# Two-step top-p graph kernel on one core: query projections set apart from the key projections, the last normalisation rounds spread over the last body, and step two's kept sums taken from a column of ones

## The chip, the core and the metric

One core of a Trainium2 chip runs the kernel. TensorE (PE), VectorE (DVE), ScalarE (ACT), GpSimd (POOL) and SyncE (SP, which issues the DMAs) each work through a stream of their own in program order and meet through semaphores. The metric is device time in microseconds (us), as a median of several runs. Lower is better.

## What is computed

The input x has 3327 rows of 128 features, adj is 3327 by 3327. Cut to what matters:

```python
def _top_p_attention(X, W1, W2, W3):
    q = X @ W1.T @ W2.T
    k = X @ W3.T
    probs = softmax(q @ k.T)                 # one row for each node
    # sort, keep the largest until their sum before them reaches 0.9
    A = probs * mask
    return A / jnp.maximum(A.sum(-1, keepdims=True), 1e-12)

R = S + eye(N); R = R / R.sum(-1, keepdims=True)
Xf = Xa = X
for n in range(2):
    A = _top_p_attention(Xa, W1, W2, W3)
    Xf = R @ Xf
    Xa = A @ Xa
    Z = Z + Xf @ U1[n].T + Xa @ U2[n].T
h = X + Z
y = (h - mean(h)) / sqrt(var(h) + 1e-5) * ln_g + ln_b
out = layernorm(x + y)
```

## The kernel before

The 3327 rows are 26 tiles of 128 and 13 pairs of tiles. A row of attention or of adj is 3328 columns wide, in 7 chunks of 512 (the last is 256). All is fp32.

**The preamble** (L549 to L565 on TensorE, L660 to L671 on ScalarE, L1155 to L1165 on VectorE) takes the features chunk by chunk. TensorE turns a chunk (L532), ScalarE copies it into `xT`, which is the tile `blkT` under another name with room for two chunks (L665). TensorE multiplies it by the key weights (L558) and by the query weights (L559). VectorE copies the keys into `kT` (L1159) and the queries into `Q`, in two halves (L1162). TensorE then makes the logits of pair 0 for the chunk before (L546, in banks 6 and 7 every time) and ScalarE stores them (L657). VectorE reads runs of them with MAX8 (L821); when all are read it takes the negated row maximum (L844, L846), and with that ScalarE starts on the exponentials (L678 for the candidates, L683 for the rows). Ahead of them in ScalarE's stream lies the copy of the turned U weights (L671), which TensorE turns at L569. Only the queries of the first chunk are read by pair 0.

**The bodies.** A unit is one tile of 128 rows of A or R times the features: 7 chunks, each turned by TensorE (L585), copied to `blkT` by ScalarE (`empty_block`, L708) and multiplied (L606), two chunks behind in step two. A body holds the two A units of a pair and some R units. TensorE's and ScalarE's streams walk through the bodies in the same order (`for b in bodies`), and the logits and exponentials of a later pair lie between the chunks of a body. Pair p's body can start when VectorE has masked its first tile.

**VectorE, pair by pair:** it waits for the exponentials, searches the threshold (`search`, L917 first), finds the ties, masks each of the two tiles (`settle`: four L1212 and one L1214, which also gives the kept sum), then takes the maximum of the kept sums with a least value (L1262) and the reciprocal (L1263). ScalarE scales with that when it empties the sums of an A unit (`store_sums`, L729), and GpSimd adds the result to `H` (`add_part`, L479). GpSimd also adds the diagonal to each loaded adj tile (L443), and finishes the R units of step one (`save`, with an inverse at L454 to L457 and a scaling at L467).

**The end.** The two layer norms of a pair are six rounds that alternate between ScalarE and GpSimd (`norm_round`; L756, L758, L760 on ScalarE, L487 to L501 on GpSimd). ScalarE does rounds at chunk 2 of a unit. The rounds that are left when the last body starts are four, all of pair 11: rounds 2 to 5. Before, ScalarE does all four ahead of the first copy of the last body, and then loads the table of the square root (L772). Rounds 2 and 5 are L760; after round 2 GpSimd runs L499, L500 and L501. The last pair's tiles are finished by VectorE (L1291 to L1301) with a square root on ScalarE for each norm (L795).

## Time and profile before

| | before |
|---|---|
| median of 3 runs | 1452.03 us (1451.74 to 1453.0) |
| the profiled execution | 1454.91 us |
| its span, first to last instruction | 1452.9 us |
| mean granted TensorE clock | 0.93 |
| PE busy | 1232.3 us, 85% |
| DVE busy | 1290.2 us, 89% |
| ACT busy | 921.8 us, 63% |
| POOL busy | 354.6 us, 24% |

A busy share is an average over stages that have different limits. The step-one bodies run from about 43 to 414 us, step two's bodies from about 531 us to the end. In the timeline a row gives the start, the duration, the engine, the line, the operation and how many instructions are merged; in brackets stands how long the engine had idled, and what it waited for. In the chain of work that ended last only the part of an instruction that nothing later covers is counted.

### The profile page before, as it was taken

The page shows a single profiled execution, that of the slowest core. Times are in us where ns is not written, and L with a number is a line of the kernel's source. Part 1 is how long each engine was busy: PE and PEld are TensorE (multiplying, and loading weights), DVE is VectorE, ACT ScalarE, POOL GpSimd, SP SyncE. Part 2 cuts the span into 40 slices and gives each one's busy share as a digit, 9 for nine tenths or more (in the row PEclk, how much of TensorE's full clock was granted, in tenths as well). Part 3 has the DMA queues.
Part 4 walks back from the last instruction along what each step waited for, and adds up shares of the span by engine and source line. Part 5 has one row for each costly group of instructions (what it writes and reads, how often), then busy time and mean ns, then how long its engine had stood idle before and what let it go on. Part 6 is the DMA issues. An engine that isn't in the chain of part 4 may idle for free.

```text
span 1452.9 us, 29724 instructions
## 1 busy us (share of the span) xinstructions
PE 1232.3 (85%) x9162; PEld 1039.4 (72%) x9162; DVE 1290.2 (89%) x7002; ACT 921.8 (63%) x1974; POOL 354.6 (24%) x584
## 2 busy tenths in 40 slices
PE   8799999999997979997999888839894938749875
PEld 3577777777785978887887777637874837647875
DVE  5789898989985899999989999999999989999992
ACT  3787888788757565655566646546765627556743
POOL 0221132123201331412132121102331314202340
PEclk9899999999998989998999898959997979969997
DMA  5000000000021541412223131402221121302230
GB/s 201 1 2 2 2 2 2 2 2 2 2 96 48 186 146 48 142 49 95 96 96 119 25 143 49 142 1 83 108 95 50 48 95 49 142 2 95 96 88 8
DMA packets 16599, 96.49 MB, mean 66 GB/s; under 512 B 1251, under 2 KB 8930, under 8 KB 9730
## 3 DMA queue, kind: packets, MB, share of 16 engines
q1 hardware_dynamic: 16384, 94.14, 18.5%
q8 instruction: 72, 1.18, 0.3%
q14 instruction: 143, 1.17, 0.3%
HBM read 92.43 MB, written 1.70 MB: 65 GB/s over the span
## 4 chain that ended last, share of the span: by engine, by line
PE 43%; DVE 37%; ACT 12%; issue 5%; POOL 2%; DVEq 1%; DMA 0%; SPq 0%; ACTq 0%; POOLq 0%
PE bank L606 24%; DVE cand L821 14%; PE bank L585 11%; DVE junkC L878 8%; PE bank L546 5%; ACT E L683 5%; ACT blkT L708 2%; DVE E L1212 2%; ACT cand L678 2%; DVE sub L1042 2%; DVE E L1214 1%; PE bank L621 1%; DVE junkS L878 1%; DVE slots L941 1%; ACT S L683 1%
## 5 line engine op out<-in xcount | busy, mean ns | idle before, releaser
L708 ACT ACTIVATE blkT<-bank 128x512 f32<-128x512 f32 (+1 forms) x728 | 406.8, 565 | 291.2 <-PE bank L585 287.3
L821 DVE MAX8 cand<-E 128x8 f32<-128x32 f32 (+1 forms) x2992 | 405.0, 192 | 36.6 <-ACT E L657 21.5
L606 PEld LDWEIGHTS bank<-X,blkT 128*128 128x128 f32 x2704 | 330.6, 192 | 112.0 <-ACT blkT L708 78.3
L606 PE MATMUL bank<-X,blkT 128*128 128x129 f32 (+1 forms) x2704 | 377.7, 282 | 17.4 <-ACT blkT L708 16.3
L585 PE MATMUL bank<-ident,S 128*128 128x128 f32 x1560 | 242.5, 275 | 16.3 <-POOL S L443 16.3
L585 PE MATMUL bank<-ident,E 128*128 128x128 f32 x1144 | 182.0, 283 | 84.2 <-DVE E L1214 84.2
L878 DVE SCALAR_TENSOR_TENSOR junkC<-cand,st 128x128 f32<-128x128 f32 (+2 forms) x390 | 243.3, 632 | 2.4
L606 PE MATMUL bank<-YF,blkT 128*128 128x128 f32 x1352 | 192.8, 287 | 40.6 <-ACT blkT L708 40.5
L606 PEld LDWEIGHTS bank<-YF,blkT 128*128 128x128 f32 x1352 | 172.3, 199 | 72.3 <-ACT blkT L708 61.2
L546 PE MATMUL bank<-kT,Q 64*128 64x512 f32 (+1 forms) x728 | 198.8, 616 | 8.2 <-ACT E L657 7.6
L585 PEld LDWEIGHTS bank<-ident,E 128*128 128x128 f32 x1144 | 142.7, 147 | 86.5 <-DVE E L1214 85.4
L585 PEld LDWEIGHTS bank<-ident,S 128*128 128x128 f32 x1560 | 186.7, 142 | 21.2 <-POOL S L443 18.4
L606 PE MATMUL bank<-YA,blkT 128*128 128x128 f32 x1352 | 187.4, 282 | 13.9 <-ACT blkT L708 13.9
L657 ACT ACTIVATE E<-bank 128x512 f32<-128x512 f32 (+1 forms) x308 | 158.2, 567 | 62.4 <-PE bank L546 61.9
L606 PEld LDWEIGHTS bank<-YA,blkT 128*128 128x128 f32 x1352 | 172.3, 199 | 14.8 <-issue 13.2
L1214 DVE SCALAR_TENSOR_TENSOR E<-E,st 128x3328 f32<-128x3328 f32 x44 | 163.6, 3733 | 8.8 <-DVE flag_i L1019 6.8
L683 ACT ACTIVATE E<-E,negm 128x1664 f32<-128x1664 f32 x88 | 147.5, 1677 | 0.0
L472 POOL TENSOR_TENSOR H<-hy,H 128x128 f32<-128x128 f32 x26 | 38.8, 1492 | 281.3 <-ACT hy L744 281.3
L1212 DVE MATCH_REPLACE8 E<-gone,E 128x832 f32<-128x832 f32 x104 | 103.8, 1009 | 0.0
L678 ACT ACTIVATE cand<-cand,negm 128x520 f32<-128x520 f32 (+1 forms) x78 | 45.0, 592 | 90.8 <-DVE negm L846 90.8
L546 PEld LDWEIGHTS bank<-kT,Q 64*128 64x128 f32 x728 | 57.2, 186 | 43.3 <-issue 27.6
L479 POOL TENSOR_TENSOR H<-part_h,H 128x128 f32<-128x128 f32 x50 | 33.8, 677 | 192.4 <-ACT part_h L729 192.4
(220 smaller groups left out, 1338.2 us busy)
## 6 DMA issues: line engine op xcount, KB each, us to landing
S<-in_adj_dram SPq DMA_DIRECT2D x50, 1663.5 KB, 7.0
S<-in_adj_dram SPq DMA_DIRECT2D x2, 1455.6 KB, 8.8
X<-in_x_dram SPq DMA_DIRECT2D x6, 256.0 KB, 4.8
out_dram<-H SPq DMA_DIRECT2D x1, 1408.0 KB
S<-in_adj_dram SPq DMA_DIRECT2D x2, 194.9 KB, 10.1
u_in<-in_L_gnn_U_dram SPq DMA_DIRECT2D x4, 64.0 KB, 9.6
out_dram<-H SPq DMA_DIRECT2D x1, 128.0 KB
w_in<-in_L_gnn_W_dram SPq DMA_DIRECT2D x2, 32.0 KB, 2.1
```

Of the source, the lines that this page charges most:

```text
L472: pool.tensor_tensor(H[:, u.t, :], hy[:, z, 0:D], H[:, u.t, :], ALU.add)
L546: pe.matmul(lg_banks(q)[xx][:, 0:LW[c]], Q[h0:h1, p, :], kT[h0:h1, s, c * BANK:c * BANK + LW[c]], start=True, stop=True).then_inc(logits_r ...
L585: m = pe.transpose(BLK[early][slot][:, b * P:(b + 1) * P], src[:, j * P:(j + 1) * P], ident[:, :])
L606: m = pe.matmul(bank[int(u.acc)][:, 0:width], blkT[:, slot, b * P:(b + 1) * P], rhs[:, j, 0:width], start=(j == 0), stop=(j == NT - 1))
L657: act.activation(E[where_e[s, p]][:, xx, c * BANK:c * BANK + LW[c]], lg_banks(q)[xx][:, 0:LW[c]], ACT.Copy).then_inc(logits_done, 1)
L678: act.activation(c, c, ACT.Exp, bias=negm[:, par, xx:xx + 1], scale=1.0, accum_out=total[:, par, xx:xx + 1])
L683: return act.activation(e[:, xx, lo:hi], e[:, xx, lo:hi], ACT.Exp, bias=negm[:, par, xx:xx + 1], scale=1.0, accum_out=Zh[:, par, xx, half: ...
L708: act.activation(blkT[:, slot, 0:w], BLK[early][slot][:, 0:w], ACT.Copy).then_inc(blk_done, 1)
L821: v.max(cand[:, par, xx, 8 * r:8 * r + 8], E[where_e[self.s, self.p]][:, xx, r * w:min((r + 1) * w, N)]).then_inc(s_max, 1)
L878: return v.scalar_tensor_tensor(out=out, in0=a, scalar=limit, in1=a, op0=ALU.is_lt, op1=ALU.mult, accum_out=total)
L1212: link.post(v.match_replace(back, gone[:, xx, k, :], back, 0.0))
L1214: v.scalar_tensor_tensor(out=e[:, xx, :], in0=e[:, xx, :], scalar=one(TSTAR, xx), in1=e[:, xx, :], op0=ALU.is_ge, op1=ALU.mult, accum_out= ...
```

## The change

Three things change.

1. In the preamble `xT` becomes a tile for all chunks (it takes the room of `YF`, not used before step one's bodies). Only chunk 0 is multiplied by the query weights at once; the other six are multiplied after the last logits of pair 0, into banks 0 to 5, and VectorE copies them after it has read the last run of pair 0. Pair 0's logits alternate between two pairs of banks. TensorE starts the bodies after the copies.
2. The four rounds of the last body are done by ScalarE behind the copies and sums of steps 0, 3, 6 and 9 of the last body's 14 chunks, and the square root's table is loaded at step 12.
3. `YA` gets a column of ones, and A units of step two (but for the last pair) multiply 129 columns. ScalarE copies sum and kept sum unscaled; GpSimd takes the maximum, the inverse (four instructions), scales the 128 columns and adds. VectorE no longer reads out the kept sum in step two and drops L1262 and L1263 there, but for the last pair. The least value goes into a tile of its own, `least`, before whose rewriting VectorE waits for `h_taken`.

```diff
-        YA = sb("YA", [P, NT, D])
+        YA = sb("YA", [P, NT, D + 1])
...
-        xT = blkT
+        xT = YF[:, :, :].rearrange("p t d -> p (t d)")
...
-        FIRST_LG = [bank[6], bank[7]]
+        FIRST_LG = [[bank[6], bank[7]], [bank[1], bank[3]]]
...
+            pool.memset(YA[:, :, D:D + 1], 1.0).then_inc(setup_done, 1)
...
             def add_part(u):
                 pool.wait_ge(sums_ready, u.k + 1)
                 if u.m:
                     pool.wait_ge(h_taken, u.m)
-                pool.tensor_tensor(H[:, u.t, :], part_h[:, u.m % 2, :], H[:, u.t, :], ALU.add).then_inc(h_taken, 1)
+                ps = part_h[:, u.m % 2, 0:D]
+                if u.kind == "A":
+                    total, d = part_h[:, u.m % 2, D:D + 1], sum_inv[:, u.x:u.x + 1]
+                    then(pool.tensor_scalar(total, total, least[:, (NPAIR + u.pair) % 2, u.x:u.x + 1], None, ALU.max))
+                    inverse(d, total)
+                    then(pool.tensor_scalar(ps, ps, d, None, ALU.mult))
+                pool.tensor_tensor(H[:, u.t, :], ps, H[:, u.t, :], ALU.add).then_inc(h_taken, 1)
...
-                pe.matmul(bank[2 * (c % 2)][:, 0:w], W3T2[:, :, :], xT[:, c % 2, 0:w], start=True, stop=True)
-                pe.matmul(bank[2 * (c % 2) + 1][:, 0:w], WqT2[:, :, :], xT[:, c % 2, 0:w],
-                          start=True, stop=True).then_inc(kq_ready, 1)
-                if c:
-                    pe.wait_ge(kq_done, 3 * c)
+                k = pe.matmul(bank[2 * (c % 2)][:, 0:w], W3T2[:, :, :], xT[:, c * BANK:c * BANK + w], start=True, stop=True)
+                if c == 0:
+                    pe.matmul(bank[1][:, 0:w], WqT2[:, :, :], xT[:, 0:w], start=True, stop=True).then_inc(kq_ready, 1)
+                else:
+                    k.then_inc(kq_ready, 1)
+                    pe.wait_ge(kq_done, c + 2)
                     logits(0, 0, c - 1)
...
+            pe.wait_ge(logits_done, 2 * NCH)
+            for c in range(1, NCH):
+                pe.matmul(bank[c - 1][:, 0:CW[c]], WqT2[:, :, :], xT[:, c * BANK:c * BANK + CW[c]],
+                          start=True, stop=True).then_inc(q_ready, 1)
             pe.wait_ge(u_loaded, 64)
-            pe.wait_ge(logits_done, 2 * NCH)
             for n in range(2 * STEPS):
                 last = pe.transpose(bank[7][:, n * P:(n + 1) * P], u_in[:, n, :], ident[:, :])
             last.then_inc(u_turned, 1)
-            pe.wait_ge(setup_done, 14)
+            pe.wait_ge(setup_done, 15)
+            pe.wait_ge(q_done, 2 * (NCH - 1))
...
             def multiply(g):
-                width = D + 1 if u.s == 0 and u.kind == "R" else D
+                width = D + 1 if (u.s == 0) == (u.kind == "R") and u.k <= last_part.k else D
...
             def store_sums(u):
-                if u.kind == "A":
-                    gp = u.s * NPAIR + u.pair
-                    act.wait_ge(inv_ready, gp + 1)
-                    scale = a_inv[:, gp % 2, u.x:u.x + 1]
+                if u.kind == "A" and u.s == 0:
+                    act.wait_ge(inv_ready, u.pair + 1)
+                    scale = a_inv[:, u.pair % 2, u.x:u.x + 1]
...
+                elif u.kind == "A":
+                    ins = act.activation(part_h[:, u.m % 2, :], ps[:, 0:D + 1], ACT.Copy)
...
             for b in bodies:
                 if b.p == NPAIR - 1 and b.s:
-                    for job in norm_rounds.get(last_part.k + 1, ()):
-                        norm_round(*job)
-                    act.wait_ge(act_round, 2 * len(norm_at))
-                    act.activation(junkA[:, 0, 0:1], ones[:, 0:1], ACT.Sqrt)
+                    for n, job in enumerate(norm_rounds.get(last_part.k + 1, ())):
+                        b.late.setdefault(len(b.seqs) - 2 - LATE_EVERY * (len(norm_rounds[last_part.k + 1]) - n), []).append(job)
...
+                    for job in b.late.get(m, ()):
+                        norm_round(*job)
+                    if b.late and m == len(b.seqs) - 2:
+                        act.wait_ge(act_round, 2 * len(norm_at))
+                        act.activation(junkA[:, 0, 0:1], ones[:, 0:1], ACT.Sqrt)
...
             def search(link, s, p, par):
+                if s and p >= 2:
+                    dve.wait_ge(h_taken, a_unit[s, 2 * (p - 2) + 1].m + 1)
+                link.post(v.tensor_scalar(least[:, par, :], z, 1e-12, None, ALU.mult))
...
+            runs.finish()
+            for c in range(1, NCH):
+                dve.wait_ge(q_ready, c)
+                queries(c, bank[c - 1], q_done)
...
+                            if s and p < NPAIR - 1:
+                                v.scalar_tensor_tensor(out=e[:, xx, :], in0=e[:, xx, :], scalar=one(TSTAR, xx), in1=e[:, xx, :],
+                                                       op0=ALU.is_ge, op1=ALU.mult).then_inc(a_ready, 1)
...
+                    if s == 0 or p == NPAIR - 1:
                         link = Chain(s_tie)
...
                         link(v.tensor_tensor(two(SUM), two(SUM), least[:, par, :], ALU.max))
                         v.reciprocal(a_inv[:, par, :], two(SUM)).then_inc(inv_ready, 1)
```

`queries` is the pair of query copies that stood in the preamble's loop.

## Rows read from the trace of the kernel before

**Rows 1.** The page's chain that ended last, shares of the span by engine.
```profile
PE 43%; DVE 37%; ACT 12%; issue 5%; POOL 2%; DVEq 1%; DMA 0%; SPq 0%; ACTq 0%; POOLq 0%
```
**Rows 2.** Busy by stretch: from:to length, then busy us and instructions by engine, PEclk, DMA.
```profile
74.00:102.00 28.00, 27.68 (x196) 20.89 (x195) 26.25 (x122) 22.59 (x46) 8.64 (x8) 1.00 0.01 2
...
676.00:744.00 68.00, 65.01 (x504) 57.64 (x502) 62.68 (x375) 42.12 (x84) 17.93 (x30) 0.96 0.28 99
...
1214.00:1300.00 86.00, 57.13 (x447) 50.47 (x446) 82.02 (x456) 46.36 (x111) 21.12 (x40) 0.84 0.17 61
```
**Rows 3.** The chain in order of time, 845 to 1300 us: start, us, what.
```profile
968.50 2.82 PE bank L585 x12
...
1291.89 2.82 PE bank L585 x12
```
**Rows 4.** Timeline of PE in the preamble: start, us, instruction, and idle before.
```profile
17.18 1.13 PE L546 MATMUL bank<-kT,Q 64*128 64x512 f32 x4
...
19.60 1.02 PE L559 MATMUL bank<-blkT,WqT 128*128 128x512 f32 x2
20.55 1.13 PE L546 MATMUL bank<-kT,Q 64*128 64x512 f32 x4
...
31.09 1.09 PE L546 MATMUL bank<-kT,Q 64*128 64x255 f32 x4 [0.60 <-DVE Q L1162]
32.74 0.63 PE L569 MATMUL bank<-ident,u_in 128*128 128x128 f32 x4 [0.56 <-ACT E L657]
```
**Rows 5.** Timeline of ACT around the first exponentials.
```profile
33.40 0.60 ACT L671 ACTIVATE UT<-bank 128x512 f32<-128x512 f32 x1 [0.81 <-PE bank L569]
35.48 0.40 ACT L678 ACTIVATE cand<-cand,negm 128x128 f32<-128x128 f32 x1 [1.48 <-DVE negm L846]
...
42.92 0.57 ACT L708 ACTIVATE blkT<-bank 128x512 f32<-128x512 f32 x1
```
**Rows 6.** Timeline of DVE at the end of the preamble.
```profile
31.03 3.96 DVE L821 MAX8 cand<-E 128x8 f32<-128x208 f32 x14
```
**Rows 7.** Busy by stretch as in rows 2, after the first exponentials' idle time.
```profile
38.50:49.00 10.50, 5.46 (x18) 3.62 (x19) 4.94 (x33) 8.48 (x14) 0.00 (x0) 0.53 0.00 1
```
**Rows 8.** Timeline of DVE where pair 9 ends and pair 10 begins.
```profile
1210.49 3.69 DVE L1214 SCALAR_TENSOR_TENSOR E<-E,st 128x3328 f32<-128x3328 f32 x1
...
1214.76 0.16 DVE L917 TENSOR_TENSOR st<-Zh 128x2 f32<-128x2 f32 x1
```
**Rows 9.** Timeline of DVE where pair 8 ends and pair 9 begins.
```profile
1125.46 0.50 DVE L1262 TENSOR_TENSOR st<-st 128x2 f32<-128x2 f32 x1
```
**Rows 10.** GpSimd lines: count, then duration in ns as min/median/max.
```profile
L454 POOL TENSOR_TENSOR row_inv<-new_x,minus_one x26: 562/569/2478, 61.1 to 853.7; 128x1 f32<-128x1 f32 x26
...
L467 POOL TENSOR_SCALAR scaled<-hy,row_inv x26: 612/612/3295, 64.7 to 857.0; 128x128 f32<-128x128 f32 x26
```
**Rows 11.** Timeline of ACT from the last part's sums to the end.
```profile
1408.99 0.37 ACT L729 ACTIVATE part_h<-bank,row_inv 128x128 f32<-128x128 f32 x1 [1.65 <-PE bank L606]
...
1421.07 1.28 ACT L772 ACT_TABLE_LOAD   x1
...
1422.47 1.55 ACT L708 ACTIVATE blkT<-bank 128x512 f32<-128x512 f32 x3
...
1440.02 0.19 ACT L795 ACTIVATE sd<-sd 128x1 f32<-128x1 f32 x1
```
**Rows 12.** Timeline of PE in the last body.
```profile
1423.19 2.04 PE L606 MATMUL bank<-YA,blkT 128*128 128x128 f32 x8 [12.99 <-ACT blkT L708]
...
1432.22 1.06 PE L606 MATMUL bank<-YA,blkT 128*128 128x128 f32 x8
...
1433.55 0.61 PE L606 MATMUL bank<-YA,blkT 128*128 128x128 f32 x4
...
1439.54 2.40 PE L606 MATMUL bank<-YA,blkT 128*128 128x128 f32 x20
```
**Rows 13.** Timeline of POOL between the parts of the last norm rounds.
```profile
1411.00 3.98 POOL L500 TENSOR_TENSOR H<-H,gb 128x256 f32<-128x256 f32 x1
```

More of the change, by code:

```diff
@@ L113, in new_body @@
         b.early, b.s, b.p, b.off = early, s, p, off
-        b.units, b.seqs, b.emit, b.exps, b.turn, b.mul, b.first_exps = [], [], {}, {}, {}, {}, []
+        b.units, b.seqs, b.emit, b.exps, b.turn, b.mul, b.first_exps, b.late = [], [], {}, {}, {}, {}, [], {}
         b.look = 1 if early else 2
@@ L181, in gnn_top_p_kernel @@
     ROUNDS = 6
+    LATE_EVERY = 3
     norm_rounds = {}
@@ L234, in gnn_top_p_kernel @@
         blkT = sb("blkT", [P, 3, BANK])
-        xT = blkT
+        xT = YF[:, :, :].rearrange("p t d -> p (t d)")
         new_x = sb("new_x", [P, 2, D + 1])
-        part_h = sb("part_h", [P, 2, D])
+        part_h = sb("part_h", [P, 2, D + 1])
+        least = sb("least", [P, 2, 2])
+        sum_inv = sb("sum_inv", [P, 2])
         scaled = sb("scaled", [P, D])
@@ L316, in gnn_top_p_kernel @@
         kq_done = sem("kq_done")
+        q_ready = sem("q_ready")
+        q_done = sem("q_done")
         kq_next = sem("kq_next")
@@ L357, in lg_banks @@
             if q < NCH:
-                return FIRST_LG
+                return FIRST_LG[q % 2]
             ring = LG[0] if q < late_logits else LG[1]
@@ L536, in logits @@
                 q = lg_seq(s, p, c)
-                before = q - (1 if q < NCH or q >= late_logits else 2)
+                before = q - (1 if q >= late_logits else 2)
                 if q in (NCH, NCH + 1):
@@ L899, in smallest_kept, with search @@
                 return w, d
-            def search(link, s, par):
+            def search(link, s, p, par):
                 n = NC[s]
@@ L1149, in drop_ties, with queries @@
                 link(v.memset(excess[:, xx, :], 0.0))
-            dve.wait_ge(setup_done, 14)
+            def queries(c, q_ps, done):
+                m = CW[c] // (2 * P)
+                for xx in range(2):
+                    h0, h1 = xx * DA, (xx + 1) * DA
+                    v.tensor_copy(Q[h0:h1, 2 * c:2 * c + m, :],
+                                  q_ps[h0:h1, 0:CW[c]].rearrange("p (m x d) -> p m x d", x=2, d=P)[:, :, xx, :]).then_inc(done, 1)
+            dve.wait_ge(setup_done, 15)
             dve.sem_clear(s_max)
@@ L1179, in _ @@
                     link = Chain(s_search, runs, fill, 8 if s else 0)
-                    search(link, s, par)
+                    search(link, s, p, par)
                     if p + 1 < NPAIR:
@@ L1213, in settle @@
                                 dve.wait_ge(s_tie, link.n)
-                            v.scalar_tensor_tensor(out=e[:, xx, :], in0=e[:, xx, :], scalar=one(TSTAR, xx), in1=e[:, xx, :],
-                                                   op0=ALU.is_ge, op1=ALU.mult, accum_out=one(SUM, xx)).then_inc(a_ready, 1)
+                            if s and p < NPAIR - 1:
+                                v.scalar_tensor_tensor(out=e[:, xx, :], in0=e[:, xx, :], scalar=one(TSTAR, xx), in1=e[:, xx, :],
+                                                       op0=ALU.is_ge, op1=ALU.mult).then_inc(a_ready, 1)
+                            else:
+                                v.scalar_tensor_tensor(out=e[:, xx, :], in0=e[:, xx, :], scalar=one(TSTAR, xx), in1=e[:, xx, :],
+                                                       op0=ALU.is_ge, op1=ALU.mult, accum_out=one(SUM, xx)).then_inc(a_ready, 1)
                     with dve.If(code < 1):
@@ L1256, in _ @@
                             settle()
-                    link = Chain(s_tie)
-                    if gp >= 2:
-                        q = gp - 2
-                        dve.wait_ge(sums_ready, a_unit[q // NPAIR, 2 * (q % NPAIR) + 1].k + 1)
-                    dve.wait_ge(a_ready, 2 * gp + 2)
-                    link(v.tensor_tensor(two(SUM), two(SUM), two(LEAST), ALU.max))
-                    v.reciprocal(a_inv[:, par, :], two(SUM)).then_inc(inv_ready, 1)
+                    if s == 0 or p == NPAIR - 1:
+                        link = Chain(s_tie)
+                        if gp >= 2:
+                            dve.wait_ge(sums_ready, a_unit[0, 2 * min(gp - 2, NPAIR - 2) + 1].k + 1)
+                        dve.wait_ge(a_ready, 2 * gp + 2)
+                        link(v.tensor_tensor(two(SUM), two(SUM), least[:, par, :], ALU.max))
+                        v.reciprocal(a_inv[:, par, :], two(SUM)).then_inc(inv_ready, 1)
             link = Chain(s_fin)
```

28 lines of the change are left out of this document (11 added, 17 removed).

## The prediction

> **What bounds the kernel now.** I read the chain of work that ended last first, then busy time by stretch, then the chain in order of time, and then the two ends instruction by instruction. The page's chain is shared between PE (43%), DVE (37%) and ACT (12%) [rows 1]: no engine bounds the kernel alone, so each part of the change is worth what the stage around it lets through. Busy time by stretch tells the stages apart [rows 2]. In a step-one body (74 to 102 us) PE is busy 27.68 of 28 us; these bodies repeat and nothing of them is changed. In the early bodies of step two (676 to 744) PE and DVE are both near 95%, and the chain there runs through TensorE and the exponentials that its order puts ahead of block copies. In a late body (1214 to 1300) DVE is busy 82 of 86 us and PE only 57. The chain in order of time [rows 3] gives the joints of that late stretch: VectorE up to 968.5, where TensorE at last gets pair 6's first masked tile; then a body of TensorE and the exponentials it leads to; VectorE again from the next search until 1291.9, where TensorE gets pair 10's first tile; and from there TensorE without a longer wait, until the last body, where it stands still for 12.99 us [rows 12].
>
> **The preamble.** A chunk now takes 3.37 us of TensorE, from one logits start to the next (17.18 to 20.55) [rows 4], and the query product with its gap is 0.95 of it (19.60 to 20.55). Without it I take 0.9 less. The first removed product lies ahead of 13.8 us, five more full ones and a half one ahead of the last logits: about 0.8 + 4 x 0.9 + 0.7 for the chunk edges = 5.1, plus the 0.60 us that the last logits waited for VectorE's query copy [rows 4]. So the last logits start near 25.5 instead of 31.09, the reading of the last runs (14 MAX8, 3.96 us [rows 6]) ends near 29.5, and the maximum is there 5 to 6 us sooner. Does ScalarE start the exponentials then? Not yet, because the copy of the U weights stands ahead of them in its stream, and TensorE makes that only behind the moved products. Before: last logits 31.09, U turned from 32.74, copied from 33.40 to 34.0, then 1.48 us of waiting for the maximum, first exponential at 35.48 [rows 4, 5]. After: last logits 25.5, stored by 26.7 to 26.8 (the same 1.6 us later), six products of 0.86, the last one half: 4.7 us, to 31.5; U turned and copied 1.3 us later, to 32.8. The exponentials start at about 32.8 and not at 35.48: **2.7 us**, rounded down to 2.6. What was removed is thus half given back; the wait that ends last is the U copy. The six pairs of query copies (5 x 0.87 + 0.6 = 4.9 us, of the kind now beside the key copies) run on VectorE from about 29.6 to 34.6 while ScalarE takes 7.44 us for the exponentials (35.48 to 42.92 [rows 5]); VectorE would idle there. TensorE's four filling jobs, which end before the exponentials with room now, start at 34.6 and end near 38.5, and the first block copy is due at 40.2. Bounds: 1.0 (the loop is held by ScalarE or VectorE at some chunk, whose copies and MAX8 add up to an estimated 1.7 and 1.9 to 2.4 us a chunk against 2.5 for TensorE) and 5.0 (if the U copy were no obstacle).
>
> **The clock behind it.** Between 38.5 and 49 us the granted clock is 0.53, that is 1.2 GHz, after TensorE idled for the exponentials, and its 5.46 us of work there are on the chain [rows 7]; at 2.4 GHz they would be 2.7. In the new order it idles in two shorter pieces, 32.0 to 34.6 for the query copies and about 1.7 us before the first block copy. Whether the clock stays up over such pieces this trace doesn't settle, so I take under half, **1.2 us**, with bounds of -1 (low clock during the filling jobs, which then end after the exponentials) and 2.7.
>
> **Step one and the early bodies of step two.** They move earlier as they are: 0. The memset of 26 ones is one more in a row of small ones before the features arrive. The 129th column is in step one's R units now; I cost it at nothing, since a tile's product there and in A units takes the same 0.22 us, with 0.4 us (24 units x 26 tiles x 4 passes of one column at 2.4 GHz is 1.0 us, less than half of it on the chain) as upper bound.
>
> **VectorE in step two.** From the end of a pair's second masking (1210.49 + 3.69 = 1214.18) to the first instruction of the next search (1214.76) are 0.58 us with L1262 and L1263 in them [rows 8]; I leave 0.13 for the semaphores, so 0.45 a pair. It counts only where VectorE carries the chain: by rows 3 that is the end of pair 5, and of pairs 8 and 9; the other ends have their slack in front of a wait on TensorE or ScalarE. 3 x 0.45 = 1.35, and 0.3 more where GpSimd had stretched L1262 to 0.50 us [rows 9]. The masking itself stays at 3.69 us for 3328 elements, 1.1 ns each; dropping its accumulator is at most the read-out, which another instruction covers. On GpSimd each of 24 A units gets a maximum, four instructions of inverse and a scaling: in its usual durations 0.2 + 0.57 + 3 x 0.19 + 0.61 + 6 gaps of 0.08 = 2.4 us [rows 10], beside 8.7 us per unit. They take something back on VectorE, about what is seen where both run: -0.35 over the 8 or so A units within VectorE's part of the chain. Sum: **1.3 us**, bounds -1 and 3.5. The wait for `h_taken` before `least` is rewritten has search's later instructions queued behind it, but it asks for the sums of two pairs ago: 0. `store_sums` loses its wait for the inverse, which came long before: 0.
>
> On that contention the Trainium skill ("GPSIMD Engine Reference", the table at its head) says that GpSimd shares its SBUF interfaces with VectorE and contends with VectorE instructions that have two SBUF inputs. The trace agrees: L1262 has two such inputs and took 0.50 us beside GpSimd's L499 [rows 9], and GpSimd's L500 took 3.98 us beside the last masking [rows 13]. It is the rule that speaks against this part of the change.
>
> **The end.** Now ScalarE empties the last part at 1408.99, does four rounds in turn with GpSimd, and loads the table (1421.07); the first block copies come at 1422.47 [rows 11], and TensorE, which had turned three chunks, multiplies from 1423.19 [rows 12]. Put aside, the copies start at 1409.3 and TensorE multiplies from 1409.9. At the high clock a chunk costs 1.33 us (1432.22 to 1433.55 [rows 12]): 0.89 of products and 0.44 of turning. What is left is 12 x 0.89 + 2 x 0.45 of products and 9 x 0.44 + 2 x 0.22 of turning = 16.0, so TensorE ends at 1425.9 instead of 1439.54 + 2.40 = 1441.94: 16.0 us sooner. (Before, the restart at low clock cost 2.9 of it.) Two things come off. The square root's table (1421.07 to 1422.47, 1.40 us) now lies between the last block copy and the first square root, which today follows the last copy at once (1440.02) and starts VectorE's serial end: -1.4. And the rounds sit among the copies. Round 2 goes behind copy 2, near 1411; GpSimd's three instructions after it end between 1414.3 and 1415.7, as the last masking may hold L500 [rows 13]; round 3 stands behind copy 5, near 1414.5, so ScalarE waits up to a microsecond and does 0.8 us of work, and copy 6, needed at 1417.7, still comes in time. Round 5 meets the same at copy 11 and delays copies 12 and 13 by 0 to 0.9. I take -0.6. The second A tile is masked at 1414.4 and asked for at 1416. The output DMA of the pairs up to 11 leaves near 1423, against an end near 1438. So **14.0 us**, bounds 9 (each round's wait comes through to TensorE, 2 us at two places, and the last copies late) and 15.5.
>
> The Trainium skill ("ScalarE: Activation LUTs", What ACT_TABLE_LOAD costs) gives some 2.66 us for a switch of tables with what follows it; by that the end would be worth 12.7. The trace shows 1.28 for the load and the next copy 1.40 us after its start [rows 11], which I use.
>
> **Sum.** 2.6 + 1.2 + 1.3 + 14.0 = 19.1 us. The profiled execution took 1454.91 us, so it would be 1435.8. The median of the runs shown is 2.9 us lower, and on it the forecast is 1452.03 - 19.1 = **1432.9 us**.
>
> **Rivals.**
> - The end gives less: ScalarE, in order, waits for GpSimd at rounds 3 and 5, TensorE and the last copies come late. For it: L500 at 3.98 us against a usual 0.73, and a masking that lies just there; against it: the ring of three blocks, two chunks of slack. 4 to 5 us less: 1437.4.
> - The start gives nothing: the U copy and a low clock during the filling jobs eat the 3.8 us. For it: U's copy behind 4.7 us of products; against it: the 7.4 us of exponentials hide the copies. 1436.7.
> - VectorE gains more than the small instructions. The Trainium skill ("Vector Engine (DVE) Microarchitecture Reference", Points that are easy to get wrong) says that this form of instruction with two fp32 inputs runs at half throughput, none of the ports being left for the accumulator's read-out. If the accumulator halved the masking's rate, a masking without it would be 1.8 us shorter, and 8 of them lie on VectorE's part of the chain: 14.4 more, 1418.5. Against it: 3.69 us for 3328 elements is 1.1 ns each, and MAX8 with one input takes 3.96 / (14 x 208) = 1.4 ns [rows 6, 8]; so the masking doesn't run at half a rate.
> - Slower: GpSimd becomes the bound. If its seven instructions per A unit are each held by VectorE's long ones, as L454, L467 and L500 are at worst (2.48, 3.30, 3.98 us), a unit's part takes over the 8.7 us that TensorE needs for a unit, and the next adj tile's diagonal and the norm rounds, queued behind, stop TensorE and ScalarE. It decides from 8.7 us per unit; at 1 us lost on each of 24 units it eats the gain, at 1.8 the time is 1452 - 19 + 43 = 1476. Against it: medians of 0.57 and 0.61 [rows 10] and POOL idle for most of the time [rows 2].
> - The change does nothing that counts: 1452.
>
> **How the numbers follow.** Forecast as summed, within 3 us: 0.56. End gives less 0.16, start gives nothing 0.12, more gain by clock or VectorE 0.10, GpSimd as bound 0.03, no effect 0.03. The range runs from 1428.5 (clock at its bound, VectorE and the end near theirs) to 1438.5 (one of the first two rivals). What a measurement of this kernel can tell from no change is about 0.2%, 2.9 us. Faster 0.95, same 0.02, slower 0.03.
>
> **What would show it.** In the profile after: logits 2.5 us apart, first exponential at 32.8 with ScalarE's U copy just before it; no or a shorter stretch of low clock at 40 to 49; L917 0.15 us after the last masking; the last body's copies 1.33 us apart directly behind the last part's sums, the table load right behind the last of them, and no clock drop. The prediction is wrong if TensorE waits for a block copy in the last body, if VectorE's maskings get shorter, or if TensorE's waits for GpSimd's diagonal grow.

## The result and the profile after

| | before | after |
|---|---|---|
| median of 4 runs, taken side by side | 1452.51 us (1451.74 to 1455.0) | 1439.34 us (1438.29 to 1440.45) |
| ratio, 95% interval | | 0.9906 [0.9889, 0.9924] |
| span of the profiled execution | 1452.9 us | 1438.7 us |
| PE / DVE / ACT / POOL busy, us | 1232.3 / 1290.2 / 921.8 / 354.6 | 1232.8 / 1289.1 / 919.2 / 445.5 |

The kernel became faster by 13.2 us; 19.1 were forecast, and 1439.3 lies above the range. The page of after, its chain by engine and two of its groups:

```profile
PE 43%; DVE 37%; ACT 12%; issue 5%; POOL 2%; DVEq 1%; DMA 0%; SPq 0%; ACTq 0%; POOLq 0%
...
L1248 DVE SCALAR_TENSOR_TENSOR E<-E,st 128x3328 f32<-128x3328 f32 x24 | 88.9, 3703 | 0.9
...
L1251 DVE SCALAR_TENSOR_TENSOR E<-E,st 128x3328 f32<-128x3328 f32 x20 | 74.5, 3760 | 7.9 <-DVE flag_i L1044 6.8
```

The chain has the same shares as before [rows 1]. L1248 is the masking without the accumulator, L1251 the one with it: mean 3703 and 3760 ns, so the rate did not change.

**The start.** Timelines of after, PE then ACT (start, us, instruction, idle before):

```profile
17.61 1.13 PE L560 MATMUL bank<-kT,Q 64*128 64x512 f32 x4
...
20.12 1.13 PE L560 MATMUL bank<-kT,Q 64*128 64x512 f32 x4
...
26.95 4.99 PE L584 MATMUL bank<-YF,WqT 128*128 128x512 f32 x12 [1.29 <-ACT E L677]
31.77 0.60 PE L588 MATMUL bank<-ident,u_in 128*128 128x128 f32 x4
```
```profile
25.26 1.64 ACT L677 ACTIVATE E<-bank 128x512 f32<-128x512 f32 x4 [0.60 <-PE bank L560]
32.41 0.60 ACT L689 ACTIVATE UT<-bank 128x512 f32<-128x512 f32 x1 [5.52 <-PE bank L588]
32.91 0.39 ACT L696 ACTIVATE cand<-cand,negm 128x128 f32<-128x128 f32 x1
...
40.33 0.58 ACT L726 ACTIVATE blkT<-bank 128x512 f32<-128x512 f32 x1
```

A chunk takes 2.51 us instead of 3.37, the exponentials start at 32.91 instead of 35.48, and the first block copy comes at 40.33 instead of 42.92 [rows 4, 5].

Not all of that is the change. Up to the second chunk's key product both kernels have the same TensorE stream, and yet it starts at 12.01 us in before and at 11.30 in after. Timelines of PE, before and then after:

```profile
9.52 1.91 PE L559 MATMUL bank<-blkT,WqT 128*128 128x512 f32 x2
...
12.01 1.02 PE L558 MATMUL bank<-blkT,W3T 128*128 128x512 f32 x2
```
```profile
9.57 1.46 PE L574 MATMUL bank<-YF,WqT 128*128 128x512 f32 x2
...
11.30 1.02 PE L572 MATMUL bank<-YF,W3T 128*128 128x512 f32 x2
```

The first pairs of products take up to 2.08 us where later ones take 1.02, and how many do so differs from execution to execution. From that key product the first exponential comes 23.47 or 23.48 us later in all four traces with the old preamble (before and the experiments e3, e4 and e9 below) and 21.41 to 21.61 us later in the nine others with the new one (e5, whose preamble differs, aside). So the change makes the start 1.9 us shorter, and 0.7 us of the difference between these two traces is luck.

**The last body.** Timeline of ACT in after, from the last part's sums:

```profile
1408.83 0.37 ACT L748 ACTIVATE part_h<-bank,row_inv 128x128 f32<-128x128 f32 x1 [1.65 <-PE bank L626]
1409.21 1.57 ACT L726 ACTIVATE blkT<-bank 128x512 f32<-128x512 f32 x3
1412.24 0.88 ACT L779 ACTIVATE H<-H,shift,rs 128x128 f32<-128x128 f32 x2 [1.46 <-POOL shift L509]
...
1423.97 0.38 ACT L726 ACTIVATE blkT<-bank 128x256 f32<-128x256 f32 x1 [0.51 <-PE bank L605]
1424.37 1.28 ACT L812 ACT_TABLE_LOAD   x1
1425.66 0.20 ACT L812 ACTIVATE u_in<-ones 128x1 f32<-128x1 f32 x1
1425.78 0.19 ACT L818 ACTIVATE sd<-sd 128x1 f32<-128x1 f32 x1
```

The first square root comes 16.95 us behind the last part's sums (1425.78 - 1408.83). Before it came 31.03 behind (1440.02 - 1408.99 [rows 11]). From it to the end are 12.9 us in both. So the end gave 14.08 us, which is 31.03 less 16.95. But the last part's sums themselves come only 0.16 us sooner: all that the start and the kept sums brought is gone by then.

There is room left in the end. Timeline of DVE in after:

```profile
1420.03 0.15 DVE L1320 TENSOR_SCALAR sd<-sd 128x1 f32<-128x1 f32 x1
1425.99 0.17 DVE L1332 RECIPROCAL rs<-sd 128x1 f32<-128x1 f32 x1 [5.81 <-ACT sd L818]
```

VectorE has the first tile's variance at 1420.18 and idles 5.81 us for its square root, which stands behind all block copies and the table in ScalarE's stream.

**Where it went.** I set the unit sums of the two traces side by side (the lead is the time in before less that in after, for the same instruction). At the second search the lead is 3.75 us (73.19 to 69.44). It then falls in three steps of 1.6 to 1.7 us. Besides these, 0.7 us go between 457 and 543 us, and the lead swings between 1080 and 1220 us and comes out of that 1.0 us larger. Two of the steps are falls of the granted clock at places where the trace of before has none. Busy by stretch of after (columns as in [rows 2]); before shows 1.00 in the last column but two of all four:

```profile
386.00:390.00 4.00, 2.29 (x15) 1.99 (x16) 3.16 (x18) 2.99 (x6) 1.13 (x1) 0.92 0.00 0
390.00:394.00 4.00, 4.00 (x18) 2.80 (x17) 3.68 (x26) 1.73 (x5) 0.73 (x2) 0.66 0.01 4
1342.00:1346.00 4.00, 1.97 (x14) 1.78 (x13) 3.86 (x31) 0.69 (x2) 2.30 (x8) 0.88 0.78 253
1346.00:1350.00 4.00, 4.00 (x27) 4.00 (x27) 3.96 (x8) 2.00 (x4) 0.43 (x1) 0.69 0.43 179
```

The lead goes from 3.8 to 2.2 over the first and from 2.5 to 0.8 over the second. The third step, from 1.1 to -0.6, is a wait at 1388 us. Timelines of after, POOL then PE:

```profile
1383.85 0.70 POOL L515 TENSOR_TENSOR H<-H,X 128x256 f32<-128x256 f32 x1
1384.54 0.30 POOL L490 TENSOR_SCALAR part_h<-part_h,least 128x1 f32<-128x1 f32 x1
1384.92 0.68 POOL L461 TENSOR_TENSOR sum_inv<-part_h,minus_one 128x1 f32<-128x1 f32 x1
...
1386.59 0.69 POOL L492 TENSOR_SCALAR part_h<-part_h,sum_inv 128x128 f32<-128x128 f32 x1
1387.37 0.45 POOL L493 TENSOR_TENSOR H<-part_h,H 128x128 f32<-128x128 f32 x1
1387.79 0.22 POOL L501 TENSOR_SCALAR mv<-mv 128x2 f32<-128x2 f32 x1
1387.97 0.46 POOL L450 TENSOR_TENSOR S<-S,ident 128x128 f32<-128x128 f32 x1
```
```profile
1388.48 0.66 PE L605 MATMUL bank<-ident,S 128*128 128x128 f32 x4 [1.51 <-POOL S L450]
```

GpSimd's new work for an A unit (2.8 us, from 1384.54 to 1387.37), itself queued behind a norm round (up to L515), stands ahead of the next adj tile's diagonal (L450), and TensorE waits for that. TensorE's next wait of this kind, for the last adj tile, gives 0.8 us back (1.18 us in after, 1.95 in before). It does so with no loss ahead of it too: e1, e2 and e3 gain 0.7 to 0.8 us on before there, so it is before's trace that has the long wait.

### The profile page after: what moved, and what is told of

It is laid out like the page before. It is cut to its first block, busy times and chain, and to the rows that moved or that the text cites. A ratio compares the mean times of both kernels' runs of the same rounds, so it can differ in the third digit from the quotient of the medians.

```text
span 1438.7 us, 29788 instructions
## 1 busy us (share of the span) xinstructions
PE 1232.8 (86%) x9162; PEld 1040.7 (72%) x9162; DVE 1289.1 (90%) x6954; ACT 919.2 (64%) x1974; POOL 445.5 (31%) x729
## 3 DMA queue, kind: packets, MB, share of 16 engines
q8 instruction: 72, 1.18, 0.3%
## 4 chain that ended last, share of the span: by engine, by line
PE 43%; DVE 37%; ACT 12%; issue 5%; POOL 2%; DVEq 1%; DMA 0%; SPq 0%; ACTq 0%; POOLq 0%
PE bank L626 24%; DVE cand L844 13%; PE bank L605 11%; DVE junkC L901 8%; PE bank L560 5%; ACT E L701 5%; ACT blkT L726 2%; DVE E L1245 2%; ACT cand L696 2%; DVE sub L1067 2%; DVE E L1248 1%; PE bank L641 1%; DVE junkS L901 1%; DVE slots L966 1%; DVE st L909 1%
## 5 line engine op out<-in xcount | busy, mean ns | idle before, releaser
L626 PE MATMUL bank<-YA,blkT 128*128 128x129 f32 (+1 forms) x1352 | 186.6, 280 | 0.5 <-ACT blkT L726 0.5
L1248 DVE SCALAR_TENSOR_TENSOR E<-E,st 128x3328 f32<-128x3328 f32 x24 | 88.9, 3703 | 0.9
L1251 DVE SCALAR_TENSOR_TENSOR E<-E,st 128x3328 f32<-128x3328 f32 x20 | 74.5, 3760 | 7.9 <-DVE flag_i L1044 6.8
```

The source lines that it names most:

```text
L626: m = pe.matmul(bank[int(u.acc)][:, 0:width], blkT[:, slot, b * P:(b + 1) * P], rhs[:, j, 0:width], start=(j == 0), stop=(j == NT - 1))
L1248: v.scalar_tensor_tensor(out=e[:, xx, :], in0=e[:, xx, :], scalar=one(TSTAR, xx), in1=e[:, xx, :], op0=ALU.is_ge, op1=ALU.mult).then_inc(a ...
L1251: v.scalar_tensor_tensor(out=e[:, xx, :], in0=e[:, xx, :], scalar=one(TSTAR, xx), in1=e[:, xx, :], op0=ALU.is_ge, op1=ALU.mult, accum_out= ...
```

## The experiments

Theory Q: what the start and the kept sums bring is lost to GpSimd's queue, the long A unit's part ahead of the diagonal. Theory C: it is lost to falls of the granted clock. "Before" and "after" are the two kernels of this case. In the diffs, - is the kernel that is named as the base.

**e1_ends**: after, with its part 3 taken back (VectorE reads out the kept sums again). The core of it:

```diff
-                if u.kind == "A":
+                if False:
                     total, d = part_h[:, u.m % 2, D:D + 1], sum_inv[:, u.x:u.x + 1]
...
-                            if s and p < NPAIR - 1:
+                            if False:
...
-                    if s == 0 or p == NPAIR - 1:
+                    if True:
```

> The changed kernel without its third part: the kept sums go through VectorE's accumulator and L1262/L1263 as before, the preamble and the last body are the changed ones. Theory Q (GpSimd's queue: the longer part of an A unit stands ahead of the next adj tile's diagonal and takes back what VectorE gains, about 1.7 us in the body of pair 11): this kernel is 1 to 3 us faster than the changed kernel, 1436 to 1438 us, and TensorE doesn't wait for the diagonal near 1388 us. Rival C (the granted clock: all of the missing 5 us are two short falls of the clock, at 389 and at 1345 us, and the third part is worth the +1.3 us forecast): this kernel is as fast as the changed one or 1.3 us slower, 1439 to 1441 us, with the same two falls. If neither holds and the sum of the two ends is all there is: 1452.5 - 17.8 = 1434.7 us.

1438.4 us, ratio 0.9899 [0.9881, 0.9916]: 1 us less than after or the same, which doesn't decide between the two theories. The wait at 1388 us is gone; the clock fall near 389 is there, the one near 1346 isn't.

**e2_start** (before with the new preamble alone), **e3_tail** (before with the new last body alone) and **e4_ksum** (before with the kept sums alone) take the same diff apart; their edits are the parts 1, 2 and 3 of the change.

> Only the preamble is changed. Both theories: VectorE's first search 2.6 us and its second 3.75 us sooner than before. Rival C: the clock falls again after the idle time of TensorE near 389 us and the gain behind it is 2.2 us. Theory Q says nothing of it. If the fall is a matter of where the idle time comes to lie and this kernel has it at the same place as the changed one, then it has the fall too: 1449.5 to 1450.5 us; without it 1448.7 us.

> Only the last body is changed. Both theories: from the last part's sums (1409.0 us, as before) to the end 14.0 us less, 1438.5 us; the trace up to 1409 as before, with no clock fall at 393 us or at 1347 us. A gain of 11 us or less would say that the end was worth less than forecast.

> Only the kept sums are changed (column of ones, GpSimd's seven instructions per A unit). Forecast +1.3 us (1451.2 us). Theory Q: VectorE's ends of pairs get 0.45 us shorter, but TensorE waits 1 to 2 us longer for the diagonal in the body of pair 11, net -0.5 to +1 us of gain. Rival C: +1.3 us, with no longer waits for the diagonal. In both the masking stays at 3.69 us without its accumulator; if it fell to 1.9 us the rule of half throughput would hold.

e2: 1452.13 us, ratio 0.9993 [0.9979, 1.0007]. e3: 1439.25, 0.9905 [0.9886, 0.9924]. e4: 1452.64, 0.9997 [0.9988, 1.0007]. Beside before's 1453.41 in the same runs, the last body alone brings 14.2 us, all that after has; the other two parts alone bring 1.3 and 0.8, neither told apart from nothing. For e2, 1448.7 was expected without a clock fall: its trace has none near 389 us and its span is 3.7 us shorter than that of before (1449.2 and 1452.9), but its median is only 1.3 below.

The traces add a warning. The preambles of before, e3 and e4 are the same code, yet their second searches are at 73.19, 72.23 and 70.97 us. The trace of before had the slowest start of the three, so leads against it are 1.0 and 2.2 us too large at the second search, and 2.0 us at the last part's sums for e3, which up to there is the same code.

**e5_shift** (theory C, a few small copies ahead of the first exponentials, to move everything behind them):

```diff
+            for n in range(3):
+                act.activation(u_in[:, n, :], ident[:, :], ACT.Copy)
+
             def exp_candidates(gp, s, xx):
```

> The changed kernel with three small copies on ScalarE (0.3 us each, 0.9 us in all) ahead of the first exponentials: dead time, by which everything behind comes 0.9 us later. Rival C (whether a short idle time of TensorE brings the clock down depends on when it falls): the first search is 1.7 us sooner than before instead of 2.6, but the clock doesn't fall near 389 us, as it did not in the kernel with the preamble alone, which stood 3.4 us ahead there; so behind 400 us it is at least as far ahead as the changed kernel (2.2 us): 2.8 to 3.0. If the fall belongs to the idle time as such, it comes again and the lead behind it is 1.3 us.

1441.01 us, 0.9907 [0.9889, 0.9924]. The clock falls near 389 us (granted 0.59 from 390 to 394) and near 1346 again, although everything was 1.6 us later than in after (0.6 by the edit, the rest by slower first products, as above). What was expected of the shift did not come; whether a fall happens is not set by such a shift alone.

**e6_diag** (theory Q, the diagonal ahead of the second A unit's part):

```diff
-            for u in units:
-                if u.kind == "R" and 1 < u.n + 1 < 2 * NT and u.n + 1 != START_R:
+            early = set()
+            for i, u in enumerate(units):
+                if u.kind == "A" and u.s and i + 1 < len(units):
+                    r = units[i + 1]
+                    if r.kind == "R" and r.n + 1 < 2 * NT:
+                        early.add(r.n)
+                        add_diagonal(r_units[r.n + 1])
+                if u.kind == "R" and 1 < u.n + 1 < 2 * NT and u.n + 1 != START_R and u.n not in early:
```

> The changed kernel with one order changed on GpSimd: in step two the diagonal of the adj tile that the second R unit of a body needs is added ahead of the second A unit's part, not behind it. Theory Q: TensorE's wait of 1.51 us at 1388 us is gone and nothing else moves, 1 to 1.5 us less from there on (about 0.7 us by the end, since the next tile's DMA then ends the wait). Rival C: no change in that wait beyond 0.3 us, as the DMA would end it.

1437.9 us, 0.9897 [0.9877, 0.9917], 1.4 us below after with overlapping intervals. Timeline of POOL in e6_diag at the same place; L450 now stands ahead of L490, and TensorE no longer waits there:

```profile
1382.29 0.47 POOL L450 TENSOR_TENSOR S<-S,ident 128x128 f32<-128x128 f32 x1
1382.72 0.31 POOL L490 TENSOR_SCALAR part_h<-part_h,least 128x1 f32<-128x1 f32 x1
```

**e7_dose** (theory Q, the inverse done three times, eight more instructions for each A unit on GpSimd):

```diff
-                    inverse(d, total)
+                    for _ in range(3):
+                        inverse(d, total)
```

> The changed kernel with the four instructions of the inverse done three times over: 8 more GpSimd instructions, about 2.3 us, in each of the 24 A units. Theory Q: TensorE's wait for the diagonal at 1388 us grows from 1.5 to about 3.8 us, waits of the same kind appear in other bodies where GpSimd does a norm round 1 or 4 and a scaling in the same unit, and VectorE loses 0.5 us or so to contention: 2 to 6 us slower than the changed kernel. Rival C: GpSimd has room, under 1 us slower.

1446.24 us, 0.9949 [0.9934, 0.9964]: 6.9 us above after, where theory Q expected 2 to 6. Timelines of POOL and PE in e7_dose:

```profile
1383.73 0.30 POOL L490 TENSOR_SCALAR part_h<-part_h,least 128x1 f32<-128x1 f32 x1
...
1390.08 0.45 POOL L450 TENSOR_TENSOR S<-S,ident 128x128 f32<-128x128 f32 x1
```
```profile
1390.58 1.11 PE L606 MATMUL bank<-ident,S 128*128 128x128 f32 x4 [7.33 <-POOL S L450]
```

The queue is a real mechanism, and at this dose a dear one. From L490 to the diagonal are 6.35 us here instead of 3.43, so 2.9 us more with the gaps between the instructions. That makes a wait of 7.33 us here, and of 4.34, 3.56 and 2.29 at three other places where after waits 0.7 or less. The lead over before tells where it costs: behind those three it comes back, to 5.3 us at 1303 us (after has 2.5), and over the wait at 1390 us it falls from 4.8 to -4.8. TensorE then restarts at half clock (granted 0.50 from 1390 to 1394). So in this trace the price of the dose is that one wait, in the stretch that TensorE carries. That doesn't show that the queue costs anything at the dose of after.

**e8_best** is e6_diag with the four rounds behind steps 0, 3, 5 and 8 and the table load at step 9:

```diff
-                        b.late.setdefault(len(b.seqs) - 2 - LATE_EVERY * (len(norm_rounds[last_part.k + 1]) - n), []).append(job)
+                        b.late.setdefault((0, 3, 5, 8)[n], []).append(job)
...
-                    if b.late and m == len(b.seqs) - 2:
+                    if b.late and m == 9:
```

> The changed kernel with the diagonal ahead of the second A unit's part, and with the last body's rounds behind blocks 0, 3, 5 and 8 and the table of the square root loaded behind block 9, where ScalarE idles 0.7 us a block. Both theories: the first square root follows the last block copy at once, 0.6 to 1.2 us less between the last part's sums and the end (12.7 to 13.3 less than before plus 1.4: the stretch that took 29.8 us takes 28.6 to 29.2). Theory Q adds 0.7 us for the diagonal: 1437.4 us in all against 1439.3; rival C only the first: 1438.3 us.

1435.66 us, 0.988 [0.9861, 0.9899]. Timeline of ACT in e8_best:

```profile
1404.24 0.37 ACT L754 ACTIVATE part_h<-bank,row_inv 128x128 f32<-128x128 f32 x1 [1.65 <-PE bank L632]
...
1417.55 1.28 ACT L818 ACT_TABLE_LOAD   x1
1418.85 0.20 ACT L818 ACTIVATE u_in<-ones 128x1 f32<-128x1 f32 x1
1418.96 0.85 ACT L732 ACTIVATE blkT<-bank 128x512 f32<-128x512 f32 x2
1419.70 0.20 ACT L824 ACTIVATE sd<-sd 128x1 f32<-128x1 f32 x1
```

The table comes ahead of the last two copies, which had room, and the square root is 15.46 us behind the last part's sums instead of 16.95. These 1.5 us are the table's 1.4 and its edges. Expected were 0.6 to 1.2.

The last four runs take one thing each away from e8_best. **e9_oldstart** has the preamble of before, **e10_nosum** the kept sums of before, **e11_nodiag** the diagonal where after has it, **e12_plain** both of the last two. The edits are those shown above, reversed.

> The kernel of e8_best with the preamble of the kernel before (the later start of the searches). Theory: the start's gain, some 2.6 us by the second search, is kept to the end, since PE is the engine that is late through most of the kernel: the time is 2 to 3 us above e8_best, so 1437.7 to 1438.7 us. Rival: the gain of the start is eaten in the bodies (an engine or a DMA with a place of its own, or the granted clock falling more often behind an earlier start): the time is within 1 us of e8_best, 1434.7 to 1436.7 us.

> The kernel of e8_best with the kept sums as in the kernel before (accumulator of the masking, maximum, inverse and scaling off GpSimd), so that only the start, the end and the moved diagonal are left. Theory: what the kept sums cost in the kernel after was GpSimd's queue ahead of the next diagonal; with the diagonal moved they should pay 1 to 2 us, so this kernel takes 1436.5 to 1437.5 us, above e8_best. Rival: what VectorE saves is off the path that sets the end, and this kernel is within 0.5 us of e8_best or below it.

> The kernel of e8_best with GpSimd's diagonal back where the kernel after has it (behind the A unit's part): kept sums on, diagonal late. Theory (GpSimd's queue): 1.0 to 2.0 us above e12_plain's gain on e8_best, that is 1436.7 to 1437.7 us, and 0 to 1 us above e12_plain, since the kept sums then pay nothing; in its trace TensorE waits over 1 us for the diagonal at one place at least behind 1200 us. Rival (the difference between the kernels after and e6_diag was scatter): within 0.5 us of e8_best, 1435.2 to 1436.2 us.

> The kernel of e8_best without the kept sums and with the diagonal late: only the start and the end of the change. With e8_best, e10_nosum and e11_nodiag it makes a square of kept sums by place of the diagonal. Theory (GpSimd's queue): without the kept sums the place of the diagonal is worth little, so 1436.5 to 1437.5 us, within 0.5 us of e10_nosum (1437.03), and not above e11_nodiag by more than 0.3 us. Rival: moving the diagonal pays by itself, kept sums or not: 1438.0 to 1438.8 us.

| | start | kept sums | diagonal | us | before beside it | ratio |
|---|---|---|---|---|---|---|
| e8_best | new | new | early | 1435.66 | 1453.59 | 0.9880 [0.9861, 0.9899] |
| e9_oldstart | old | new | early | 1437.69 | 1453.77 | 0.9893 [0.9875, 0.9910] |
| e10_nosum | new | old | early | 1437.03 | 1453.77 | 0.9890 [0.9872, 0.9908] |
| e11_nodiag | new | new | late | 1435.71 | 1452.97 | 0.9882 [0.9866, 0.9899] |
| e12_plain | new | old | late | 1435.35 | 1452.97 | 0.9882 [0.9866, 0.9899] |

e9 and e10 came out where the first of their two expectations had them, 2.0 and 1.4 us above e8, though the intervals overlap. e11 and e12, which test theory Q, did not. In the trace of e11 TensorE waits 0.69 us for the late diagonal, at 1385.5. (Its wait of 1.16 us at 1395.5, for the last adj tile, is no sign of the late diagonal: e6 and e8, with the early one, have 1.20 and 1.77 there.) Yet e11 is as fast as e8 by its ratio, and so is e12, with neither. In the four traces with kept sums and a late diagonal (after, e4, e5, e11) the wait is 1.51, 0.91, 1.25 and 0.69 us, far from the 5 to 6 us that are missing, and no median shows a price for it. So theory Q falls as the explanation of what is missing in after; a price of up to 1 us isn't excluded.

**All executions together.** I fitted one base and five additive terms to the 108 executions of before, after and ten of the experiments (all but e5 and e7; the scatter left over is 1.6 us):

| part | effect, us | standard error |
|---|---|---|
| new start | -0.9 | 0.4 |
| kept sums from the column | -0.3 | 0.4 |
| new last body | -14.0 | 0.5 |
| diagonal early | +0.4 | 0.6 |
| rounds at 0, 3, 5, 8 and table at 9 | -2.4 | 0.6 |

The base is 1453.6 us. The fit takes the parts as additive and the executions as independent; both are assumptions. The last row is more than the 1.5 us that the trace of e8 shows; the rest of it is not explained.

**The clock and the scatter.** Each execution is listed with its span and mean granted clock. For the 44 executions of before beside the experiments the time and the clock go together with a correlation of -0.91, from 1451.5 us at 0.932 to 1458.05 at 0.926, some 0.8 us for each 0.001. From stretches of 4 us between 50 and 1404 us I added up (1 - granted clock) x length: 85.4 us in before, 90.4 in after, 85.3 in e3, 87.1 in e4, 90.5 in e1, 88.7 in e6, 88.8 in e9, 85.3 or 85.4 in e2, e8, e10, e11 and e12. The differences come in steps of 1.6 to 1.8 us, one fall more or less. The fall near 389 us is in after, e1, e5 and e7, not in e2, e6, e8, e10, e11, e12, nor in the four traces with the old preamble. One near 1346 is in after, e5 and e9 alone. The part of theory C that stands: in the trace of after two falls took 3.3 us of the lead, and traces of one code differ by such falls. That they make the scatter of all executions is argued from the correlation, not shown. Also not shown: that the change causes them. Kernels with the same preamble have them and have them not, and the mean over the eight traces with the new preamble (e5 and e7 aside) is 87.0 us against 86.6 for the four with the old one.

## Why the prediction was wrong, step by step

The forecast was 6.4 us low. By the fit it splits into 2.9 for the start, 1.0 for the kept sums, 1.6 for the base and 1.0 for four executions of after that lay above the fit (1439.3 against 1453.6 - 0.9 - 0.3 - 14.0 = 1438.4). The end is right to the tenth.

**The start, 2.6.** The mechanism came true: a chunk of 2.51 us, the U copy just ahead of the exponentials, and these at 32.91 (32.8 forecast). The first search is at 40.56 instead of 43.15, 2.59 sooner. But that agreement is in part luck. Counted from the second chunk's key product, up to which the code is the same, the first search comes after 31.13 to 31.15 us in the four old traces and 29.07 to 29.26 us in the new ones: 1.9 us. The term was 0.7 too large.

**The clock behind it, 1.2.** Busy by stretch of after:

```profile
38.50:49.00 10.50, 8.04 (x43) 5.80 (x44) 7.74 (x51) 8.20 (x16) 0.00 (x0) 0.84 0.00 1
```

0.84 instead of 0.53 [rows 7], and the lead grows by 1.16 to 3.75 by the second search: right for this pair of traces. From the first search to the second are 28.76 to 28.89 us in the new traces and 30.04, 29.70, 29.34 and 29.56 in the old, so over all of them the term is 0.8.

**What failed is the step behind these two: "They move earlier as they are: 0".** A lead of 3.75 us at the second search was to reach the end whole. Two things were wrong with that. First, there was less to carry. The second searches of the kernels with the new start, e5 aside, lie between 68.88 and 69.94 us, those with the old one (before, e3, e4, e9) at 73.19, 72.23, 70.97 and 71.83: by the means the start is worth 2.5 us there (2.7 counted from the key product), not 3.8. Second, behind it the clock falls at some places in some executions and not in others, 1.6 to 1.7 us each, and the waits shift. At the last part's sums the same two groups (e5 and e7 aside) are 1.9 us apart (leads of 0.16, 1.77, 4.51, 3.81, 4.75, 4.14, 3.15 and 4.22 against 0, 1.97, 1.59 and 2.28). Over all executions the start is worth 0.9 us with an error of 0.4; by single pairs of medians it is 1.3 (e2 and before), 0.9 (e1 and e3) and 2.0 (e8 and e9). Between 1 and 2 us is what the runs bear out, of 2.5. That part of the lead is lost on the way is what the fit says; between the two groups of traces the loss of 0.6 us is within their scatter. For after's own trace the places are shown. Why the mean loss is what it is stays open.

**The kept sums, 1.3.** The working for VectorE was nearly right: its small step from the last masking to the next search is shorter, and in e4 its lead grows from 3.00 at pair 5's search to 5.19 at pair 11's. Timeline of DVE in after:

```profile
1207.66 3.69 DVE L1248 SCALAR_TENSOR_TENSOR E<-E,st 128x3328 f32<-128x3328 f32 x1
1211.27 0.41 DVE L940 TENSOR_TENSOR st<-Zh 128x2 f32<-128x2 f32 x1
```

From masking to search are 3.61 us instead of 4.27 [rows 8], 0.66 less, and the first instruction of the search takes 0.41 us instead of 0.16 beside GpSimd. The step that failed is the one that carries "3 x 0.45 = 1.35" and the 0.3 to the end: from 1291.9 us TensorE carries the chain [rows 3], yet I counted VectorE's gain at pairs 8 and 9 as kept, and put no price on who waits behind GpSimd's new work in its queue, which stood only in the rival with 0.03. The reading "without a longer wait" was wrong too: the trace of before waits there 1.18, 2.02 and 1.95 us for adj tiles (at 1336.5, 1347.4 and 1398.7 us). In e4 TensorE's lead in that stretch is 3.8; it loses 1.9 of it between 1363 and 1373 us, where the clock is low for longer than in before, and 1.1 at a wait of 0.91 us for the diagonal, and has 1.59 at the last part's sums, less than e3, without the kept sums, has there (1.97). The measured effect, -0.3 with an error of 0.4, is within the bounds of -1 and 3.5 but not at the value taken.

**The masking.** The rival by which the masking without accumulator would be 1.8 us shorter is refuted: 3703 ns beside 3760. The rule in the Trainium skill ("Vector Engine (DVE) Microarchitecture Reference", Points that are easy to get wrong) gives half throughput to this form with two fp32 inputs; the trace shows 1.1 ns an element with and without the read-out, and the measurement decides.

**GpSimd as the bound** had 0.03. Its mechanism, the diagonal queued behind a longer A part, is in after at one place (1.51 us) and not at every unit. e7 shows how near it was: 2.9 us more for each unit's part cost 6.9 us.

**The end, 14.0.** 14.08 in the traces, 14.2 by e3, 14.0 by the fit. TensorE doesn't wait for a block copy: it is busy for all of 1405 to 1425 us at full clock. Busy by stretch, then a timeline of PE:

```profile
1405.00:1425.00 20.00, 20.00 (x182) 19.89 (x180) 10.26 (x21) 13.42 (x36) 9.78 (x19) 1.00 0.28 81
```
```profile
1420.89 0.60 PE L605 MATMUL bank<-ident,E 128*128 128x128 f32 x4
...
1422.22 0.60 PE L605 MATMUL bank<-ident,E 128*128 128x128 f32 x4
```

These are 1.33 us a chunk (1420.89 to 1422.22), as taken from [rows 12]. The stretched instruction came at another place than L500: L509 took 3.45 us beside the masking (L1251, 3.71 us from 1408.45), and round 2 waited 1.46 us for it. That agrees with what the Trainium skill ("GPSIMD Engine Reference", the table at its head) says of GpSimd and VectorE instructions with two SBUF inputs. TensorE's two chunks of slack took the wait up. The table's 1.4 us between the last copy and the first square root were there, and e8 shows that they needn't be. (The aside that the restart at low clock cost 2.9 us comes to 2.75 by its own numbers, 1441.94 - 1423.19 less 16.0; no term hangs on it.)

**The base and the range.** The forecast stands on the median of three runs, 1452.03 us. The 44 later executions of before scatter over 6.5 us, with the clock, and their median is 1453.4. The range had no term for these 1.4 us, nor one for a lead that is lost on its way.

## What to carry to other kernels

A wait removed right ahead of the end is kept whole: the 14 us of the last body came out to the tenth, since nothing stood behind it that could take them back. A lead won at the start has over a thousand microseconds of waits and clock falls ahead of it; here 1 to 2 us of 2.5 arrived. Don't read such a lead from one execution: measure it from the last instruction that both kernels share, which here took 0.7 us of luck out of 2.6. Work moved to an idle engine is free only until the next thing in that engine's queue is late: look for who waits for that, put short things that another engine needs ahead of long ones, and price it with a larger dose before believing either side. A wait seen in a trace is not yet a loss in the median (1.5 us here), and of four longer ones in e7 only the one in the stretch that TensorE carries was lost.

## What the runs showed of the chip

The time of an execution goes with its mean granted clock (correlation -0.91 over 44 executions of one kernel), and what the clock lacks in a trace, added up, comes in steps of 1.6 to 1.8 us (85.3, 87.1, 88.7, 90.4), one fall of TensorE's clock from 2.4 to 1.2 GHz more or less. The first products of an execution take up to 2.08 us for a pair that later takes 1.02, for a time that moved the second chunk by 1.5 us between traces of the same code (10.50 in e4, 12.01 in before); the granted clock from 7.5 to 12 us reads 1.00 in both, so that row doesn't explain it. The same code shows the fall near 389 us in one trace and not in another (after and e11, granted 0.66 and 1.00). A masking of 3328 elements (two fp32 inputs) takes 3.70 us whether or not it feeds an accumulator. On GpSimd, an instruction of 0.20 us took 3.45 us beside such a masking.
